# One language-model tower on one core: another order on TensorE and VectorE, and a GpSimd recurrence in two blocks

## What is computed

```python
def step(carry, inp):                         # over 128 tokens t, per head, per state n of 16
    z, y = carry
    z = (z + d * (Bu - A * y)) / (1.0 + d * d * A)
    y = y + d * z
    out = einsum('bhpn,bn->bhp', y, C_t)
yout = scan(step) + D_skip * uh
x = x + (yout * silu(zgate)) @ out_proj_w.T + out_proj_b
x = x + gelu(rms(x) @ fc1_w.T + fc1_b) @ fc2_w.T + fc2_b
```

## Time and profile before

| | us |
|---|---|
| Median of 3 runs | 1468.62 (1467.59 to 1469.27) |
| Profiled execution, its own time | 1464.07 |
| Span of its instructions | 1462.2 |
| PE busy | 1184.4 (81%) |
| DVE busy | 1160.4 (79%) |
| POOL busy | 819.6 (56%) |
| ACT busy | 757.9 (52%) |
| Mean granted PE clock | 0.915 of full |

### The profile page before, as it was taken

How to read it: one execution, slowest core, us unless ns; L and a number is a source line. 1 busy time by engine, 2 the same in 40 slices (tenths; PEclk the granted TensorE clock), 3 DMA queues, 4 the chain that set the end, 5 groups by cost and what they waited for, 6 DMA issues and landing times. The chain is left out here.

```text
span 1462.2 us, 25531 instructions
## 1 busy us (share of the span) xinstructions
PE 1184.4 (81%) x7199; PEld 814.6 (56%) x7206; DVE 1160.4 (79%) x2087; ACT 757.9 (52%) x1108; POOL 819.6 (56%) x2326
## 2 busy tenths in 40 slices
PE   0694043498989898989898989899999999898767
PEld 0352021357575756676767666666666675757444
DVE  4899933678888889888888989888888978878268
ACT  4667352354637373828273737473736555451247
POOL 7860027574757566575757575757575757560100
PEclk9999996599989899989899989998989989999889
DMA  9999400000001010101000000000000000000015
GB/s 367 408 407 425 160 23 16 12 19 16 23 10 31 1 32 3 30 6 26 10 22 16 16 16 16 16 16 16 16 16 16 16 16 16 18 17 1 0 42 188
DMA packets 62068, 92.22 MB, mean 63 GB/s; under 512 B 9101, under 2 KB 55010, under 8 KB 57554
## 3 DMA queue, kind: packets, MB, share of 16 engines
q1 hardware_dynamic: 58386, 82.10, 15.8%
q0 software_dynamic: 3072, 8.39, 1.5%
q10 hardware_dynamic: 576, 1.31, 0.2%
HBM read 81.29 MB, written 10.49 MB: 63 GB/s over the span
## 5 line engine op out<-in xcount | busy, mean ns | idle before, releaser
L747 POOL TENSOR_TENSOR stp<-Gs,X 128x32 f32<-128x32 f32 x1024 | 290.4, 284 | 263.1 <-ACT X L722 152.9
L749 POOL TENSOR_TENSOR Gs<-Gs,stp 128x32 f32<-128x32 f32 x1024 | 286.6, 280 | 80.3
L1048 PE MATMUL bank<-mT,w_fc 128*128 128x512 f32 x512 | 236.3, 599 | 7.9 <-ACT mT L1036 7.9
L604 PE MATMUL bank<-xT,w_in 128*128 128x512 f32 x512 | 235.8, 610 | 8.0 <-DVE uT L851 8.0
L1067 PE MATMUL bank<-w_fc,gl 128*128 128x256 f32 x1024 | 236.5, 379 | 0.0
L1067 PEld LDWEIGHTS bank<-w_fc,gl 128*128 128x128 f32 x1024 | 193.4, 190 | 59.8 <-issue 37.5
L837 ACT ACTIVATE uT<-bank,cols 128x512 f32<-128x512 f32 x64 | 49.5, 778 | 276.6 <-PE bank L604 276.6
L604 PEld LDWEIGHTS bank<-xT,w_in 128*128 128x128 f32 x512 | 97.7, 196 | 117.6 <-issue 107.1
L1048 PEld LDWEIGHTS bank<-mT,w_fc 128*128 128x128 f32 x512 | 95.7, 192 | 100.1 <-issue 94.7
L952 PE MATMUL bank<-MT,utok 128*64 128x128 f32 x1024 | 112.1, 408 | 45.5 <-DVE MT L938 45.4
L851 DVE SCALAR_TENSOR_TENSOR uT<-bank,cols,uT 128x500 f32<-128x500 f32 (+1 forms) x192 | 135.1, 736 | 3.0 <-ACT uT L837 0.7
(11 more groups left out here) (171 smaller groups left out, 1899.8 us busy)
## 6 DMA issues: line engine op xcount, KB each, us to landing
ring<-in_table SPq DMA_DIRECT2D x32, 1536.0 KB, 20.9
d_rep<-d_rows SPq DMA_DIRECT2D x128, 64.0 KB, 2.7
out<-res SPq DMA_DIRECT2D x16, 512.0 KB, 2.9
b_rep<-bc_rows SPq DMA_DIRECT2D x128, 32.0 KB, 1.8
c_rep<-bc_rows SPq DMA_DIRECT2D x128, 32.0 KB, 1.8
w_fc<-in_w_fc SPq DMA_DIRECT2D x2, 1024.0 KB, 8.8
w_in<-in_w_in ACTq DMA_DIRECT2D x1, 1088.0 KB, 5.2
h<-in_table,ids POOLq DMA_INDIRECT x64, 9.8
```

The lines of the kernel that those rows point to most:

```text
L604: last = pe.matmul(dst, w_in[:, k, c0:c1], xT[:, k, :], start=(k == 0), stop=(k == KD - 1))
L747: pool.tensor_tensor(stp[:], Gs[:, t, ::-1, :], X2[:, t, :, :], ALU.mult).then_inc(rec.sem, 1)
L749: pool.tensor_tensor(Gs[:, t + 1, :, :], Gs[:, t, :, :], stp[:], ALU.add).then_inc(rec.sem, 1)
L1048: last = pe.matmul(pj[n % 4][:, :], w_fc1[:, k, n * P:(n + 1) * P], mT[:, k, :], start=(k == 0), stop=(k == KD - 1))
```

## The change

**POOL.** Gs gets a dimension of RB = 2 blocks of BL = 32 steps. Block 1 starts from the unit state, so both blocks advance in the same instruction of 64 elements, and 32 steps do what 64 did. After them `pool_join` multiplies block 1 by the state at the end of block 0, a complex product: two instructions of 1056 elements in each partition and two of 528. The halves of 32 steps become halves of 16.

**PE.** The four transposes of u (`pe_u_T`) move between the last fc2 products. The first scores stand ahead of the last fc2, in other banks (tb and pj[2], pj[3] in place of sbk). u of tiles 0 and 1 stands between the second scores and the second scan output, u of tiles 2 and 3 between that and the output product.

**DVE.** The order of the turn's middle changes: row statistics of the next group ahead of the first masks, `dve_h2` behind them, skip and gate apart, `dve_stats3` and `dve_mean3` behind the last gate, the layer norm (`dve_layer_norm`, L907) moved from ahead of the reciprocal to behind `dve_mean3`, and the convolution of u ahead of `dve_bc`.

```diff
-            for t in steps:
-                if t:
-                    pool.wait_ge(rec.sem, rec.at(g, 2 * t))
-                pool.tensor_tensor(stp[:], Gs[:, t, ::-1, :], X2[:, t, :, :], ALU.mult).then_inc(rec.sem, 1)
-                pool.wait_ge(rec.sem, rec.at(g, 2 * t + 1))
-                pool.tensor_tensor(Gs[:, t + 1, :, :], Gs[:, t, :, :], stp[:], ALU.add).then_inc(rec.sem, 1)
+                pool.tensor_tensor(Gs[:, 1, 0, :, :], unit[:], unit[:], ALU.mult).then_inc(rec.sem, 1)
+            X4 = X2[:].rearrange("p (b t) a l -> p b t a l", b=RB)
+            for t in steps:
+                pool.wait_ge(rec.sem, rec.at(g, 2 * t + 1))
+                pool.tensor_tensor(stp[:], Gs[:, :, t, ::-1, :], X4[:, :, t, :, :], ALU.mult).then_inc(rec.sem, 1)
+                pool.wait_ge(rec.sem, rec.at(g, 2 * t + 2))
+                pool.tensor_tensor(Gs[:, :, t + 1, :, :], Gs[:, :, t, :, :], stp[:], ALU.add).then_inc(rec.sem, 1)
+        def pool_join(pool, g):
...
+            pool.wait_ge(rec.sem, rec.at(g, n))
+            pool.tensor_tensor(turned[:], Gs[:, 1, :, ::-1, :], b, ALU.mult).then_inc(rec.sem, 1)
+            pool.wait_ge(rec.sem, rec.at(g, n + 1))
+            pool.tensor_tensor(Gs[:, 1, :, :, :], Gs[:, 1, :, :, :], a, ALU.mult).then_inc(rec.sem, 1)
+            pool.wait_ge(rec.sem, rec.at(g, n + 2))
+            pool.tensor_tensor(Gs[:, 1, :, 0, :], Gs[:, 1, :, 0, :], turned[:, :, 0, :], ALU.subtract).then_inc(rec.sem, 1)
+            pool.tensor_tensor(Gs[:, 1, :, 1, :], Gs[:, 1, :, 1, :], turned[:, :, 1, :], ALU.add).then_inc(rec.sem, 1)
...
-        score_bank = (sbk[0], sbk[1], tb[0], tb[1])
+        score_bank = (tb[0], tb[1], pj[2], pj[3])
...
+                    if second and n == FT + 2:
+                        pe_scores(pe, p, 0)
...
+                    pe_scan_out(pe, p, 0, 0)
+                    pe_scan_out(pe, p, 0, 1)
+                    pe_scores(pe, p, 1)
+                if first:
+                    pe_u(pe, g, (0, 1))
+                if second:
+                    pe_scan_out(pe, p, 1, 0)
+                    pe_scan_out(pe, p, 1, 1)
+                if first:
+                    pe_u(pe, g, (2, 3))
```

More of the change, by code:

```diff
@@ L48 @@
 CL = LEN // CH
+RB = 2
+BL = CL // RB
 SC = G * CH
@@ L823, in dve_queries, with pe_u @@
                                          ALU.mult, ALU.mult).then_inc(q_ready.sem, 1)
-        def pe_u(pe, g):
-            for f in range(UT):
+        def pe_u(pe, g, tiles):
+            for f in tiles:
                 if since(g):
@@ L1156, in turn @@
                         pe_fc1(pe, m, n, p if second else None)
-                    if second and n == FT + 1:
+                    if second and n == FT:
                         pe_u_T(pe, p, g if first else None, 0)
                         pe_u_T(pe, p, g if first else None, 1)
+                    if second and n == FT + 1:
+                        pe_u_T(pe, p, g if first else None, 2)
+                        pe_u_T(pe, p, g if first else None, 3)
+                    if second and n == FT + 2:
+                        pe_scores(pe, p, 0)
                     if third and n >= LEAD:
@@ L1237, in turn @@
                     dve_keys(dve, p)
-                    dve_layer_norm(dve, p)
                     dve_inverse(dve, p)
                     dve_queries(dve, p)
-                if third:
-                    dve_h2(dve, m)
-                if second and nxt:
-                    dve.wait_ge(quant.sem, quant.at(g + 1))
+                if nxt:
+                    dve_row_stats(dve, g + 1)
                 if second:
@@ L1249, in turn @@
                 if third:
+                    dve_h2(dve, m)
+                if second:
+                    dve_skip(dve, p, (0, 1))
+                    for hh in range(4):
+                        dve_mask(dve, p, 1, hh)
+                    dve_gate(dve, p, (0, 1))
+                    dve_skip(dve, p, (2, 3))
+                    dve_gate(dve, p, (2, 3))
+                if third:
                     for j in range(G):
                         dve_stats3(dve, m, j)
+                    dve_mean3(dve, m)
                 if second:
-                    dve_gate(dve, p, (0, 1))
-                    for hh in range(4):
-                        dve_mask(dve, p, 1, hh)
-                if nxt:
-                    dve_row_stats(dve, g + 1)
-                if second:
-                    dve_gate(dve, p, (2, 3))
-                if third:
-                    dve_mean3(dve, m)
-                if first:
-                    dve_bc(dve, g)
+                    dve_layer_norm(dve, p)
                 if first:
                     dve_conv_u(dve, g, (0, 1))
+                    dve_bc(dve, g)
                 if nxt:
```

79 lines of the change are left out of this document (43 added, 36 removed).

## The result

| | before | after |
|---|---|---|
| Median of 4 runs | 1468.11 (1463.13 to 1469.27) | 1569.02 (1567.86 to 1569.90) |
| Profiled execution, its own time | 1464.07 | 1567.86 |
| Span | 1462.2 | 1566.1 |
| Mean granted PE clock | 0.915 | 0.911 |

The changed kernel takes 1.069 times as long, 95% interval 1.067 to 1.072. The forecast was 1586, within 1432 to 1640.

The account below looks back on a forecast made before the run. PE was taken as the bound, with DVE's chain close behind. Turns of 66.9 + 9 + 3.1 = 79.0 us, +125 over 14 turns, less 6 and 1, gave 1582 profiled, 1586 as median, range 1432 to 1640.

Parts of the forecast that it names:

- fc1 to the end of the first scores: First stretch of a turn on PE, 29.9 us at full clock, with the first scores one fc2 earlier.
- To the end of the mean: Stretch from first scores to the end of `dve_mean3`: 13.2 us of DVE work plus waits and drains, 15.0 us.
- To the normaliser: Stretch on DVE from the mean to the normaliser, layer norm added, waits for the output product gone: 14.5 us.
- What POOL does: POOL's 64-element instructions at 0.32 us; second half waits for the mean, so join and normaliser meet.
- The delay: Normaliser on DVE held up by six long POOL instructions: 9 us a turn, within 5 to 11.8.
- The clock at fc1: PE idles ahead of the transposes, so they, the small product and fc1's start slow: 3.1 us, bounds 0.9 and 4.5.
- Sum: One whole turn: 66.9 + 9 + 3.1 = 79.0 us, 8.9 more than 70.1.
- 14 turns: The 8.9 us a turn taken 14 times, from first scores of turn 2 to those of turn 16: +125 us.
- Filling and end: Filling gains 6 us net from the shorter recurrence; the end, without u, gains about 1.
- The rival of no hindrance: Join and normaliser don't hinder each other: 66.9 us a turn, 1414, or 1438 if the clock still falls; chance 0.17.
- The rival of a join behind the normaliser: Slower POOL steps put the join after the normaliser, meeting bk: about 70 a turn, 1460 to 1480 us; chance 0.12.
- The rival that the clock falls in the thin part: Scan outputs and second scores slow despite the dense products: 84 us a turn, 1655; chance 0.08.

Follow-up runs that it names:

- e7: Changed kernel without the join, and with the residual waiting until the next turn's tokens are quantised (output not the model's); 1423.26 us, 0.973 of before.
- e6: Changed kernel with the join left out, the residual's two long POOL instructions kept in place (output not the model's); 1480.31 us, 1.012 of before.
- e4: Changed kernel with the join's four and the residual's two long POOL instructions cut into four pieces each; 1489.54 us, 1.015 of before.
- e2: Changed kernel with the recurrence of 64 single steps as before and no join, only the new order kept; 1428.47 us, 0.975 of before.
- e1: Changed kernel with one wait added: the join starts only when the same turn's normaliser has ended; 1490.07 us, 1.017 of before.
- e9: Changed kernel with join before the third stage's root, residual after next quantising, step norm's short steps ahead of layer norm; 1493.45 us, 1.018 of before.
- e12: Changed kernel with u behind second scan output, blocks and join in turn 0 alone, residual waiting for last key product; 1432.71 us, 0.979 of before.

## Why the prediction was right, point by point

- **fc1 to the end of the first scores**, 29.9: measured 30.0, at full clock.
- **To the end of the mean**, 15.0: measured 15.6. The scan output at full clock takes 1.97 (taken at 2.0), and the clock stays at 1.00 in the thin part. The 0.6 are mostly DVE's waits for scores and scan output: 0.17 left of the first, 0.68 and 0.95, together 1.8 where 1.3 were counted. A slip in the sum has 0.1 more: 13.86 less 1.8 and plus 1.27 is 13.3, not 13.2.
- **To the normaliser**, 14.5: measured 14.7. The waits for the output product are gone as said, but it ends at 840.5, 2.4 us before DVE's first addition (842.92), not some 9.
- **What POOL does.** An instruction of 64 elements takes 0.318 us in the median, and 0.320 in the reversed form (taken at 0.32; before, with 32 elements, 0.252 and 0.253). POOL is idle 8.43 us ahead of `pool_rstd3`, released by the mean. The join starts 14.5 behind that (834.05 to 848.50), 0.4 us ahead of the normaliser. One detail was wrong: the recurrence starts 19.1 us behind fc1, as said, but it is released by the last key product (the row with 25.39 above), not by X.
- **The delay**, 9 within 5 to 11.8: measured 10.0. The 9 was a choice between two cases, one step in each gap (11.8) or two (6.4), and not a sum. Two to four steps were to be done when the join starts; none was, since it starts 0.4 ahead of the first and not 0.2 to 0.9 behind it. Measured were six held steps, three that slipped through in the gaps, and three behind. e7, e6 and e4 show that this term is the wait for the long POOL instructions: it is gone with them, smaller with fewer, and smaller with shorter ones.
- **The clock at fc1**, 3.1: this term was mis-sized, by 2.4. The stretch from the normaliser's end to fc1 grew from 4.9 to 5.6, by 0.7, and fc1 itself ran at 1.00. I had let fc1 start at 0.50 for 4.4 us. But PE idled from 851.0 to 863.5, the clock fell at 853.3, long before PE had work again, and it was back at 866.9, 0.2 us ahead of fc1. It had only the transposes and the small product to slow (1.97 and 1.83 us, before 1.09 and 1.08). The meeting causes hardly any of these 0.7: in e7, without it, PE idles 2.2 us ahead of the transposes, the clock stands at 0.50 from 777.9 to 781.3 (fc1 starts at 781.2), and the stretch takes 5.5.
- **Sum**, 79.0: measured 78.5. It is this near by luck: the errors nearly cancel, +0.1, +0.6, +0.2, +1.0, -2.4. The cause is right, the clock's term four times too large.
- **14 turns.** Taking +8.9 fourteen times gave 125; measured are 110.7 from the first scores of turn 2 to those of turn 16. The last of these intervals lies in turn 15, in which nothing of a next group is prepared: DVE reaches the normaliser 1.6 us ahead of the join there (1396.28 against 1397.91), nine of its steps are done by then, and only two long instructions hold a step. It cost 4.5 (71.85, before 67.31), and the other thirteen 8.2 each.
- **Filling and end**: -6 and -1. The first scores came at 268.1 in place of 279.8, 11.7 earlier, the next interval took 4.2 longer: -7.5. The rest, from those of turn 16 to the end, is +0.7.

The rival of no hindrance (1414, or 1438 with the clock's fall) names the time of a kernel without the meeting rather well: e2 took 1428, e7 1423. It failed by its condition alone: the delay was 10, not under 3. The rival of a join behind the normaliser didn't come about either (the join starts 0.4 ahead), and e1 shows that its price was too low. The rival that the clock falls in the thin part did not come about (1.00 from 816.6 to 831.9).

## What to carry to other kernels

In these runs a long GpSimd instruction and a chain of short dependent VectorE steps took turns: the chain paid the rest of one GpSimd instruction for nearly every such instruction that it met (12.6 us beside six of them, 6.4 beside two, 2.3 beside none). Before GpSimd work is made into fewer, longer instructions, look at what VectorE does at that moment, and at whether the GpSimd work was on the path at all: here it was not (a turn takes 68.1 us with 64 single steps, 42 us of POOL work, and 68.2 with half as many steps and no join), so that shortening it could gain the filling at most. If long ones are needed, look for a place beside VectorE instructions that took no longer for them here, which were the convolution steps with an operand in PSUM (0.72 to 0.74 us, e9), the maximum (1.22, e1) and the reciprocal (6.54, e12), or cut them into pieces (in four, the normaliser took 6.4 in place of 12.6, e4); and check what stands behind them, since a place that is free for one of them moves the next one onto something else.
